# A ternary feed-forward kernel on one Trainium2 core: first stage reordered, a thirteenth place for x, three loads issued by ACT

## The reference

```python
c = einsum('bct,bcd->bdt', x, weights[conditions])        # x: 128 x 64 x 512
def ternarize(W):
    delta = 0.05 * max(abs(W)); mask = abs(W) > delta
    alpha = sum(abs(W) where mask) / max(sum(mask), 1)
    return alpha * sign(W) * mask
h = gelu(c @ ternarize(W1).T + b1)                        # 8192 rows, 512 -> 2048
y = h @ ternarize(W2).T + b2                              # 2048 -> 512
scale = max(abs(y)) / 7 + 1e-8
out = x + clip(round(y / scale), -7, 7) * scale
```

## Time and profile before

| | |
|---|---|
| time, median of 3 runs | 1014.34 us |
| the profiled execution's own time | 1013.76 us |
| its span | 1012.0 us |
| PE busy | 928.2 us (92%) |
| DVE busy | 647.5 us (64%) |
| ACT busy | 546.2 us (54%) |
| POOL busy | 145.4 us (14%) |
| mean granted clock of PE | 0.97 |

### The profile page before, as it was taken

How to read it: one execution, slowest core, us unless ns; L and a number is a source line. 1 busy time by engine, 2 the same in 40 slices (tenths; PEclk the granted TensorE clock), 3 DMA queues, 4 the chain that set the end, 5 groups by cost and what they waited for, 6 DMA issues and landing times.

```text
span 1012.0 us, 14566 instructions
## 1 busy us (share of the span) xinstructions
PE 928.2 (92%) x5088; PEld 439.1 (43%) x5088; DVE 647.5 (64%) x1025; ACT 546.2 (54%) x688; POOL 145.4 (14%) x187
## 2 busy tenths in 40 slices
PE   2899999999999999999999999999999999999600
PEld 2354444444444444444444444444444444444200
DVE  7999666566667666665667666565666665633492
ACT  5685826455472827446372827446372826535290
POOL 1420030210303030110303030110303030000000
PEclk9999999999999999999999999999999999999855
DMA  9401201111210301121210301121210301105899
GB/s 347 136 9 38 46 11 42 47 47 41 52 41 17 76 10 41 46 47 41 52 41 10 83 10 41 45 48 41 52 41 10 75 18 42 42 0 201 300 394 391
DMA packets 24317, 77.85 MB, mean 77 GB/s; under 512 B 3952, under 2 KB 4080, under 8 KB 23792
## 3 DMA queue, kind: packets, MB, share of 16 engines
q1 hardware_dynamic: 20032, 73.41, 24.1%
q0 software_dynamic: 3840, 3.94, 1.4%
q10 hardware_dynamic: 432, 0.34, 0.1%
HBM read 60.89 MB, written 16.78 MB: 77 GB/s over the span
## 4 chain that ended last, share of the span: by engine, by line
PE 83%; issue 9%; DVE 4%; ACT 1%; DMA 1%; DVEq 0%; POOL 0%; POOLq 0%
PE ps L426 41%; PE ps L436 36%; PE ps L491 3%; PE ps L406 3%; ACT y L680 1%; DVE st L814 1%; DVE wts L1017 1%; DMA condb<-in_itok_B 1%; DVE y L1017 0%; DVE y L833 0%; PE ps L414 0%; PE ps L454 0%; DVE yc L746 0%; DVEq L58 0%; DVE st L697 0%
## 5 line engine op out<-in xcount | busy, mean ns | idle before, releaser
L426 PE MATMUL ps<-yc,wts 128*128 128x512 f16 x2048 | 446.3, 380 | 3.6 <-DVE yc L746 3.6
L436 PE MATMUL ps<-wts 128*128 128x512 f16 x1792 | 391.4, 379 | 0.0
L426 PEld LDWEIGHTS ps<-yc,wts 128*128 128x128 f16 x2048 | 200.7, 98 | 246.8 <-DVE yc L746 4.1
L730 DVE SCALAR_TENSOR_TENSOR wts<-g,st,wts 128x512 f16<-128x512 f32 x256 | 186.3, 749 | 144.0 <-ACT wts L593 142.4
L588 ACT ACTIVATE g<-ps,b1t,st 128x512 f32<-128x512 f32 x256 | 197.9, 773 | 129.0 <-PE ps L426 120.7
L436 PEld LDWEIGHTS ps<-wts 128*128 128x128 f16 x1792 | 173.4, 98 | 204.9
L593 ACT ACTIVATE wts<-g,st 128x512 f16<-128x512 f32 x256 | 180.8, 712 | 0.0
L575 ACT ACTIVATE xs<-yx,st 128x2048 f16<-128x2048 f32 x28 | 56.1, 2002 | 135.5 <-DVE st L764 135.5
L359 POOL PARTITION_ALL_REDUCE st<-st x46 | 22.7, 494 | 672.5 <-DVE st L699 412.7
L343 POOL DMA_INDIRECT wg<-in_L_cond_weights,ids x112 | 110.0, 982 | 41.5 <-issue 29.1
L735 DVE SCALAR_TENSOR_TENSOR y<-ps,st,b2b 128x512 f32 (+1 forms) x56 | 41.6, 747 | 78.9 <-PE ps L436 78.1
(11 more groups left out here) (127 smaller groups left out, 359.3 us busy)
## 6 DMA issues: line engine op xcount, KB each, us to landing
yx<-in_x SPq DMA_DIRECT2D x56, 512.0 KB, 6.2
out<-wts SPq DMA_DIRECT2D x12, 512.0 KB, 14.9
wts<-in_x SPq DMA_DIRECT2D x10, 512.0 KB, 5.6
y<-in_L_ffn_W SPq DMA_DIRECT2D x8, 512.0 KB, 8.6
wts<-in_x SPq DMA_DIRECT2D x4, 1024.0 KB, 5.2
y<-in_L_ffn_W SPq DMA_DIRECT2D x4, 1024.0 KB, 18.5
y<-in_x SPq DMA_DIRECT2D x4, 1024.0 KB, 10.7
out<-y SPq DMA_DIRECT2D x4, 1024.0 KB, 15.3
```

Of the source, the lines that this page charges most:

```text
L426: last = nc.tensor.matmul(psH[:, j % HB, :], T1T[:, j // HC, k, j % HC * P:(j % HC + 1) * P], csp[:, a, k, :], start=(k == 0 and a == 0), ...
L436: last = nc.tensor.matmul(psY[:, r % 2, :], hsp[:, a, j, r * P:(r + 1) * P], T2T[:, j, :], start=(j == 0 and a == 0), stop=(j == HT - 1 an ...
L730: nc.vector.scalar_tensor_tensor(out=hsp[:, 1, j, :], in0=g[:, j % HB, :], scalar=s_h, in1=hsp[:, 0, j, :], op0=ALU.mult, op1=ALU.subtract ...
```

## The change

Four things are different.

1. **Memory.** The small tiles (`wg`, `ws`, `condb`, `idx`, `ids`, `idsd`, `twos`) become parts of one tile `odd` of 1 MB, `ones` is gone. Once the last block's conditioning is done, `odd` is a thirteenth place for x (XS = 13); the blocks that are handled in halves are now 11 and 12.
2. **Closing stage.** x of blocks 13, 14 and 15 is loaded by ACT, after its rounding passes of blocks 2, 3 and 4, each behind a wait for `o_made`. SP issues only stores there.
3. **First stage, up to the first product.** The maximum over x of block 0 on DVE becomes a sum of absolute values on ACT (`dump_x`, `x0_summed`); `cscale_ready` comes behind fewer operations; `first(0, 0)` needs only one tile of W1 (`t1_begun`), and the conditioning of block 1 stands behind `first(0, 0)`. Its result goes into `cf1`, a part of y, not into g. x of block 1 is loaded ahead of W2.
4. **First stage, behind that.** DVE takes the four maxima of W2 and its first ternary quarter earlier; the second product of block 0 starts as soon as two accumulators are there; `relu2` stands behind the last gelu; `count2` multiplies the mask as the stationary operand by one column of twos, 64 products of 1 column for 16 of 512, and its result is added up with the others by the same reduction.

```diff
+            nc.vector.memset(wdirect, 0.0).then_inc(diagonal_cleared, 1)
+            nc.vector.memset(twos[:, :], 2.0).then_inc(consts_made, 1)
             dve.wait_ge(cond_loaded, 16)
...
+            act.wait_ge(xdirect_loaded[0], 16)
+            nc.scalar.activation(dump_x, xdirect[0]..., ACT.Abs, accum_out=xwb[:, 0:1])\
+                .then_inc(x0_summed, 1)
...
             mask_w1(0)
+            dve.wait_ge(wd_gathered[0], 16 * RT)
+            nc.vector.tensor_reduce(xwb[:, 1:2], wg[:, 0:RT, :], AX.XY, ALU.max, ...).then_inc(xwb_part, 1)
             mask_w1(1)
-            nc.vector.tensor_reduce(xwb[:, 0:1], xdirect[0], AX.XY, ALU.max, ...).then_inc(xwb_part, 1)
             mask_w1(2)
...
-            ternary1(0)
+            ternary1(0, slice(0, 1), t1_begun)
             low_c0(0, psC)
             low_c0(1, psC0)
+            ternary1(0, slice(1, HC))
...
             def count2(c):
-                for n in range(WCH):
-                    last = nc.tensor.matmul(psN2, twos[:, :], quarter(neg2, c, n), ...)
+                for n in range(QUARTER // P):
+                    at = c * QUARTER + n * P
+                    last = nc.tensor.matmul(psN2, neg2[:, at:at + P], twos[:, 0:1], ...)
...
+            pe.wait_ge(t2_made, 1)
+            for j in range(2):
+                pe.wait_ge(h_split, j + 1)
+                for r in range(2):
+                    second_of_first(j, r)
+            for r in range(2, RT):
+                pe.wait_ge(g_made, HT - RT + r + 1)
+                for j in range(2):
+                    second_of_first(j, r)
...
+            later = {LAST_OF[b + 2]: b for b in range(NB - XS)}
             for i, piece in enumerate(PIECES):
                 if i not in BY_VECTOR:
                     nc.scalar.activation(y_piece(*piece), ..., ACT.Identity, scale=qi, bias=magp)
+                if i in later:
+                    b = later[i]
+                    act.wait_ge(o_made, LAST_OF[b] + 1)
+                    act.dma_start(x_piece(b + XS, ALL, ALL), ...).then_inc(xt_loaded[b + XS], 16)
```

More of the change, by code:

```diff
@@ L219, in build @@
         xwb_part, xwb_all = sem("xwb_part"), sem("xwb_all")
+        x0_summed = sem("x0_summed")
         mask1_made = sem("mask1_made")
@@ L299, in _ @@
             sp.wait_ge(c_made, 2 * NB)
-            load_tail(0)
+            for b in range(2):
+                load_tail(b)
             sp.wait_ge(h_summed, NB * HT - HT // 2)
-            load_tail(1)
+            load_tail(2)
             sp.wait_ge(h_summed, NB * HT)
-            for b in range(2, 4):
+            for b in range(3, 5):
                 load_tail(b)
@@ L345, in gather, with gather_direct @@
                         in_offset=bass.IndirectOffsetOnAxis(ap=ids[:, j:j + 1], axis=0)).then_inc(w_gathered[j // HALF], 16)
-            def gather_direct(b):
-                for r in range(RT):
+            def gather_direct(b, tiles):
+                for r in tiles:
                     nc.gpsimd.indirect_dma_start(
@@ L364, in _ @@
             all_max(max1_part, 1, m1r, m1, max1_all)
+            gather_direct(1, range(2, RT))
+            pool.wait_ge(x0_summed, 1)
             all_max(xwb_part, 1, xwbr, xwb, xwb_all)
-            gather_direct(1)
             pool.wait_ge(sum1_part, 1)
@@ L452, in count2 @@
             def count2(c):
-                for n in range(WCH):
-                    last = nc.tensor.matmul(psN2, twos[:, :], quarter(neg2, c, n), start=(c == 0 and n == 0),
-                                            stop=(c == WCH - 1 and n == WCH - 1))
+                for n in range(QUARTER // P):
+                    at = c * QUARTER + n * P
+                    last = nc.tensor.matmul(psN2, neg2[:, at:at + P], twos[:, 0:1], start=(c == 0 and n == 0),
+                                            stop=(c == WCH - 1 and n == QUARTER // P - 1))
                 if c == WCH - 1:
@@ L472, in _, with second_of_first @@
                 first(0, j, wait_bank=j >= HB, wait_c=False)
[L474 to L481, removed]
+                if j == 0:
+                    pe.wait_ge(xdirect_loaded[1], 16)
+                    pe.wait_ge(w_spread, 2)
+                    condition_direct(1, 0, psC)
+                    condition_direct(1, 1, psC0)
+            pe.wait_ge(c_copied, 2)
+            def second_of_first(j, r):
+                for a in range(2):
+                    last = nc.tensor.matmul(psY0[r], hsp[:, a, j, r * P:(r + 1) * P], T2T[:, j, :],
+                                            start=(j == 0 and a == 0), stop=(j == HT - 1 and a == 1))
+                if j == HT - 1:
+                    last.then_inc(y_summed, 1)
+            pe.wait_ge(t2_made, 1)
[7 more added lines that the diff above has]
+                    second_of_first(j, r)
+            for j in range(2, HT):
                 if j % HC == 0:
@@ L489, in _ @@
                 for r in range(RT):
[L490 to L494, removed]
+                    second_of_first(j, r)
             for j in range(HT):
                 if j in (2, 3):
-                    pe.wait_ge(y_stored, j + 1)
+                    pe.wait_ge(y_stored, j - 1)
                 first(1, j)
@@ L903, in _ @@
             dve.sem_inc(delta2_ready, 1)
+            dve.wait_ge(relu_summed, WCH)
             ternary2(0)
-            for j in range(12, HT):
+            for j in range(9, 12):
                 low_h(0, j)
             ternary2(1)
-            max_c(1, link)
+            low_h(0, 12)
             ternary2(2)
+            low_h(0, 13)
+            max_c(1, link, cf1)
+            ternary2(3)
+            for j in range(14, HT):
+                low_h(0, j)
             nc.vector.tensor_scalar(ph0, ph, 1.0 / TOP, None, ALU.mult)
@@ L971, in _ @@
             tile_y, slot = tiles_of(0)
-            for r in range(RT):
+            for r in (2, 3, 0, 1):
                 store_y(0, r, tile_y(r), psY0[r])
+            dve.wait_ge(y_stored, RT)
             for r in range(RT):
```

168 lines of the change are left out of this document (81 added, 87 removed).

## The result

| | before | after |
|---|---|---|
| median | 1014.42 us (4 runs) | 1003.87 us (4 runs, 1003.67 to 1003.92) |
| profiled execution | 1013.76 us | 1003.67 us |
| its span | 1012.0 us | 1001.7 us |
| PE begins `first(0, 0)` | 33.08 | 28.54 |
| PE begins `first` of block 1 | 97.05 | 89.98 |

The ratio is 0.9894, 95% interval 0.9877 to 0.9912. The changed kernel run again, beside other kernels, gave 1003.67 beside 1014.35, ratio 0.9897 (0.988 to 0.9913). The forecast was 1005.9 in 1003.9 to 1008.8: right in direction and mechanism, and short by 2.0 us, just outside the range.

What follows compares the result with a forecast made beforehand. PE, busy for 92% of the span, was taken to bound the kernel up to its last product, and bytes moved the closing stage. 6.0 + 2.5 = 8.5 us off the median 1014.34 gave 1005.9, 8-in-10 range 1003.9 to 1008.8.

Steps and rivals of the forecast that it cites:

- second chain: First stage, DVE's list from 29.05 us: it makes the gelus late, tile 14 done at 62.65 and 15 at 64.0.
- Cover behind: After block 0's second product: yscale at 89.5, accumulators moved before PE wants them, 1.4 us to spare.
- closing stage: End of the kernel, bound by bytes: a thirteenth place moves 1.05 MB of loading earlier, 2.5 us; ACT's issuing priced nothing.
- start of the first product: First stage: earlier masks and scale, then low parts of 2.47 us, start `first(0, 0)` at 29.05, not 33.08: 4.0 us.
- fall of the clock that is spared: First products: with PE's wait cut from 3.6 to about 0.6 us the clock stays up, 1.7 us.
- count of W2's mask: Block 0's second product: 64 one-column products take 1.9 us where the old count took 3.45, 1.55 us less.
- new waits for gelus: Block 0's second product, started early, waits 0.65 us for gelu 14 and 0.5 for gelu 15: 1.15 us lost.
- the poor stretch: Closing stage near 961 us, DMA at 160 GB/s: loads on another queue might gain 0 to 1 us, taken as 0.
- A: Count of W2's mask: small products aren't fed fast enough, 6.3 us by load time; 1010.3, half way 1008; chance 0.15.
- D: Count of W2's mask: one-column products run one behind the other, 291 ns each, 18.6 us; 1022.6, slower; chance 0.04.
- B: First stage: scale comes 1.2 us late through POOL's gathers and reduction, perhaps 1.7 more by clock; 1007.1 to 1008.8; chance 0.10.
- C: Closing stage: the thirteenth place brings nothing, as DVE or ACT would bound the stage; 1008.4; chance 0.05.

Runs made afterwards that it cites:

- low9_first: The changed kernel with the low part of hidden tile 9 ahead of W2's first ternary quarter on DVE; 1003.19 us.
- low9_gather3: The changed kernel with tile 9's low part ahead of W2's first ternary quarter and three, not two, of block 1's gathers ahead of W1's maximum; 1003.09 us.
- first_quarter_whole: The changed kernel with W1's first ternary quarter made whole ahead of the low parts of c, as before the change; 1004.12 us.

## Why the prediction fell short

**What held.** Behind the last gelu, at 63.3 us, PE waits for nothing up to its last product, and the gain of the first stage went whole through the blocks behind it (7.07 us at 89.98, 7.02 at the first rounding pass). Between `first(0, 0)` and that gelu DVE's list sets when the gelus come, as the prediction's second chain had it; there an earlier start of PE isn't worth its full length, and an edit of DVE's list alone (`low9_first`) gains 0.5 us. No fall of the clock behind the first product: right. The second product waits twice for gelus: right, in place and size (1.0 us for 1.15). Cover behind: right, `yscale` was there at 87.9. The closing stage is bound by bytes: right, and the place is worth 2.5 us by the end of the full stretch and 2.6 to 2.7 by the medians, for 2.5.

**What failed.** The mechanism stood. Terms of the sum were mis-sized, all on the same side, above all the closing stage and the start of the first product:

| term | forecast, us | measured, us |
|---|---|---|
| start of the first product | 4.0 | 4.54 |
| fall of the clock that is spared | 1.7 | 1.7 |
| count of W2's mask | 1.55 | 1.85 |
| new waits for gelus | -1.15 | -1.0 |
| closing stage | 2.5 | 3.28 |
| from the profiled executions to the medians | 0 | 0.25 |

The measured column adds up to 10.6, for 10.55 between the medians.

1. *Start of the first product and DVE's list.* DVE's masks began 0.98 us earlier, at 18.66, and not 0.66 (19.0). POOL's gathers ended at 22.8 and not 22.2, and its reduction took 0.33 us and not 1.23, so DVE went on at 23.18 and not 23.4. These two misses, 0.6 late and 0.9 early, belong together, and that they nearly cancel is luck: a reduction that starts earlier lies beside a mask and takes 1.46 (`low9_gather3`). The rest came from passes rounded up (from there to the first product 5.36 us for 5.65); the prediction's own last step, 26.4 + 2.47, gives 28.9 and not 29.05. With it the whole of DVE's list came earlier: the last gelu was done at 63.3 for 64.0. Here too the prediction's terms add up to less than it says, 60.3 and not 60.5 for low part 9. The count took 1.6 for 1.9. Together 1.0 us: block 1 at 89.98 for 91.0.
2. *The closing stage.* The step that failed is the one that counted only the place. Who issues the loads was taken at 0 with 0 to 1 as its bounds, and is worth 0.3 us by the traces, 0.4 to 0.5 by the medians; the row of the poor stretch (160 GB/s at a share of 0.97) was read as saying nothing. The other 0.5 of the 0.78 is the tail behind the full stretch, 1.7 us in the trace of before and 1.2 in that of after, for which the prediction had no term. Its cause stays open.
3. *Carrying over to the median.* The profiled execution of before lies 0.66 under its median, that of after 0.2. Of this 0.46, 0.21 lies outside the spans (1.76 us before, 1.97 after); spans differ by 10.3, medians by 10.55: 0.25. That is less than the medians of the kernel before differ by from group to group.

1.02 + 0.78 + 0.25 = 2.05, of which the last 0.25 is no firmer than the scatter. The range's lower end left 2.0 us for surprises, but was put together as if the bounds of the single terms (1 us for the stretch, some tenths for the start) couldn't come true at once. But for the end of the gathers, the choices in the sum were the cautious ones, and then they add.

**The rivals.** A and D fell with 25 ns per product, in a row of 64 and of 256. B fell as a rival: the gathers did end late, at 22.8, but the reduction was short behind them; what their lateness cost is about the 0.3 us that `low9_gather3` got back. C fell: without the place 2.6 us are lost. What I had no rival for is the clock behind small products; in the change's row of 64 (1.6 us) it doesn't fall, at 256 it does.

## What to carry to other kernels

Where one engine runs without a gap for the rest of the kernel, look for what starts it, and count a wait of PE of some 3.6 us twice, once for itself and once for the clock behind it (1.7 us in both kernels that had such a wait; behind waits of 1.85 and 0.9 us it stayed up). Before valuing an earlier start, run the other engines' lists forward to where they next meet it: 1.6 us of PE's start were worth 0.6. And when a sum is made of cautious terms, put its range around the sum of the middles.

## What was not expected of the hardware

- A row of 256 products of one column took the granted clock to 0.50 although PE was shown as busy throughout, and the products behind paid 2.1 us. The same 256 in four groups with 8 long products between them did not.
- PE's idle time in the timeline understates a wait: 0.42 + 0.24 us shown, 1.0 us lost, as `first_quarter_whole` confirms.
- A reduction over partitions on POOL took 0.33 us alone and 1.23 and 1.46 us beside DVE's mask pass; a gather 0.94 alone, 1.59 and 2.41 there. DVE goes on right behind the reduction each time, so these are no artefacts of POOL's rough spans.
- Behind the last full stretch of DMA 1.0 to 1.4 us pass up to the end of the span in the twelve traces with ACT issuing the late loads, 1.7 to 2.5 in the four with SP, with a microsecond or so at 20 to 40 GB/s in the three longest.
